# A gated-delta layer: the triangular inverses from 16x16 blocks on GpSimd and three joins on TensorE, with a wave of distance

## The reference

```
L      = -(k*beta) k^T * decay        strictly lower triangular
attn   = inverse of (I - L)
v_new  = attn (v*beta) - attn (k*beta*exp(g)) state
out    = (q*exp(g)) state + ((q k^T) * decay, lower triangular) v_new
state  = state*exp(g_last) + (k*exp(g_last - g))^T v_new
```

## Time and profile before

| | us |
|---|---|
| median of three runs | 3206.09 (3205.75 to 3207.62) |
| the profiled execution's own time | 3207.93 |
| its span | 3206.1 |

### The profile page before, as it was taken

One profiled execution on the slowest core, in us unless ns is written; L12 is line 12 of the kernel. 1 busy time (PEld: TensorE's weight loads), 2 busy tenths in 40 slices (PEclk: granted clock), 3 DMA queues, 4 the chain that ended last, 5 costly groups with the idle time before them and its releaser, 6 DMA issues. The chain is left out here.

```text
span 3206.1 us, 59779 instructions
## 1 busy us (share of the span) xinstructions
PE 2795.5 (87%) x25220; PEld 1858.5 (58%) x25220; DVE 1640.8 (51%) x3069; ACT 1096.7 (34%) x2104; POOL 222.2 (7%) x203
## 2 busy tenths in 40 slices
PE   6697999969979586589999999999999999999988
PEld 3235444435324343477777777777777777777773
DVE  1633555545531422466466556646655665665541
ACT  1261111100421221344444444444444444444431
POOL 1300111100020022000000000000000000000000
PEclk8798999989989797799999999999999999999999
DMA  1001110010010000000000000000000000000000
GB/s 44 1 0 69 40 39 25 15 31 1 1 41 0 25 25 25 11 12 11 8 11 12 8 11 15 12 8 12 12 8 12 15 11 8 11 12 8 2 5 13
DMA packets 39684, 50.31 MB, mean 16 GB/s; under 512 B 5904, under 2 KB 28816, under 8 KB 39312
## 3 DMA queue, kind: packets, MB, share of 16 engines
q1 hardware_dynamic: 39440, 46.73, 4.6%
HBM read 45.68 MB, written 1.05 MB: 15 GB/s over the span
## 5 line engine op out<-in xcount | busy, mean ns | idle before, releaser
L874 PE MATMUL ps<-all_xn,f_w 128*128 128x512 f32 x640 | 287.7, 594 | 1.9 <-ACT f_share L892 1.9
L1374 PE MATMUL ps<-all_xn,a_w_qkv 128*128 128x512 f32 x512 | 256.4, 626 | 0.0
L1801 DVE SCALAR_TENSOR_TENSOR a_qkv<-a_raw,a_cur_taps,a_qkv 128x1024 f32<-128x1024 f32 x192 | 245.6, 1279 | 1.5
L1468 PE MATMUL ps<-a_inv_half,a_powers 64*64 64x64 f32 x5120 | 219.8, 220 | 0.2 <-DVE a_inv_half L1849 0.2
L1662 ACT ACTIVATE a_powers<-ps 128x512 f32<-128x512 f32 x208 | 124.2, 597 | 260.5 <-PE ps L1460 260.5
L1849 DVE TENSOR_TENSOR a_inv_half<-a_inv_half,ps 128x256 f32<-128x256 f32 x256 | 106.8, 417 | 207.3 <-PE ps L1468 207.3
L874 PEld LDWEIGHTS ps<-all_xn,f_w 128*128 128x128 f32 x640 | 122.2, 191 | 155.8 <-issue 155.8
L1468 PEld LDWEIGHTS ps<-a_inv_half,a_powers 64*64 64x64 f32 x5120 | 186.3, 134 | 11.0 <-issue 10.6
L1782 POOL TENSOR_TENSOR a_rstd<-a_var,a_half 128x4 f32<-128x4 f32 x64 | 64.4, 1007 | 1801.2 <-DVE a_var L1883 1801.2
L897 ACT ACTIVATE f_act_h<-ps 128x512 f32<-128x512 f32 x80 | 47.8, 597 | 374.5 <-PE ps L874 374.5
L1456 PE MATMUL ps<-a_powers 64*64 64x64 f32 x3584 | 174.0, 224 | 0.3 <-DVE a_powers L1807 0.3
(11 more groups left out here) (263 smaller groups left out, 5256.9 us busy)
## 6 DMA issues: line engine op xcount, KB each, us to landing
f_w<-in_f_w SPq DMA_DIRECT2D x24, 512.0 KB, 4.5
a_w_qkv<-in_a_w SPq DMA_DIRECT2D x16, 512.0 KB, 3.7
a_w_z<-in_a_w SPq DMA_DIRECT2D x16, 256.0 KB, 2.7
a_w_out<-in_a_wo SPq DMA_DIRECT2D x16, 256.0 KB, 2.7
f_w<-in_f_w SPq DMA_DIRECT2D x24, 128.0 KB, 2.3
f_index_in<-in_f_index SPq DMA_DIRECT2D x1, 2144.0 KB, 12.1
all_x<-in_x_t SPq DMA_DIRECT2D x1, 1024.0 KB, 4.8
a_wq<-in_a_wq SPq DMA_DIRECT2D x2, 512.0 KB, 3.9
```

Of the source, the lines that this page charges most:

```text
L874: mm = pe.matmul(ps[:, bank + n % 2, :], w[:, v, k, f * P:(f + 1) * P], xn[:, k, b * T:(b + 1) * T], start=k == 0, stop=k == KC - 1)
L1374: mm = pe.matmul(ps[:, to, :], w_qkv[:, k, mt * P:(mt + 1) * P], xn[:, k, b * T:(b + 1) * T], start=k == 0, stop=k == KC - 1)
L1468: mm = pe.matmul(halves(BUP)[t, r, :], powers[t, n % 2, u, r, :], inv_half[t, r, :], start=True, stop=True)
L1801: dve.scalar_tensor_tensor(to, rows, tap, to, ALU.mult, ALU.add).then_inc(conv_ready if j == TAPS - 1 else conv_step, 1)
```

## The change

Only `delta_attention` and its constants change. Each 128x128 triangle is now inverted in blocks of 16, then joined to 32, 64 and 128.

- VectorE makes v0(w+1) as before. SyncE (`spread`) stores it whole in DRAM (256 KB), copies the blocks beside the diagonal in four small DMAs, waits for the store, and reads the eight 16x16 diagonal blocks of each matrix back with four DMAs in runs of 64 bytes, so that one block lies in one partition: 32 partitions of 256 elements.
- GpSimd (`substitute`) adds the identity and does 14 steps of forward substitution, each a multiplication and an addition that wait for each other, and then writes a transposed copy: 29 two-input instructions and one copy, each waiting for the one before.
- SyncE (`gather`) waits for that, stores the result with eight DMAs in runs of 64 bytes to DRAM, waits for them, and loads it back with one DMA of 64 KB.
- VectorE (`widen`) spreads the 16-wide blocks to 32 columns. TensorE joins: `join_a`, `close_a` (32x32 operands), `join_b`, `close_b` (32x32), `join_c`, `close_c` (64x64), with six small copies by ScalarE and VectorE and an addition between them.
- The five squarings, the five updates, the transposition of v0 and their copies are gone. The loops over heads are written out; tables of the current head's gates and taps are no longer copied.
- The recurrence of wave w-1 stays in iteration w, but its normalised output is turned and projected in iteration w+1: the loop runs from -1 to 65. Three buffers replace two for at, qg, v_row and k_row.
- The weight DMAs stand in the same SyncE queue, ahead of `gather(w)` and `spread(w+1)`, with waits for work of earlier iterations.

```diff
+                def spread(w):
+                    sp.wait_ge(v0_ready, PR * (w + 1))
+                    sp.dma_start(v_dram[w % 2, 0:P * PR * P].rearrange("(p r c) -> p r c", p=P, r=PR),
+                                 v0[:, w % 2, :, :]).then_inc(v0_stored, 16)
...
+                    for k in range(4):
+                        of = slice(k * HP, k * HP + SB)
+                        sp.dma_start(v0_off[of, w % 2, :, SB:],
+                                     v0[of, w % 2, :, k * HP + SB:(k + 1) * HP]).then_inc(off_loaded, 16)
+                    sp.wait_ge(v0_stored, 16 * (w + 1))
...
+                    for r in range(PR):
+                        sp.dma_start(l16[r * NB:(r + 1) * NB, w % 2, :].rearrange("b (j c) -> b j c", j=SB),
+                                     blocks[:, :, r, 0:SB]).then_inc(l_loaded, 16)
+                def gather(w):
+                    sp.wait_ge(sub_done, w + 1)
+                    rows = t_dram[w % 2].rearrange("(b j) k r c -> b j k r c", b=NB)
+                    for r in range(PR):
+                        for k in range(2):
+                            sp.dma_start(rows[:, :, k, r, :],
+                                         z16[r * NB:(r + 1) * NB, w % 2, k, :].rearrange("b (j c) -> b j c", j=SB)
+                                         ).then_inc(t_stored, 16)
+                    sp.wait_ge(t_stored, 128 * (w + 1))
...
+                    sp.dma_start(t_narrow[:, :, :, :], t_dram[w % 2]).then_inc(t_loaded, 16)
...
+                    if made(w):
+                        gather(w)
+                    if made(w + 1):
+                        spread(w + 1)
...
+                def substitute(w):
+                    pool.wait_ge(l_loaded, 64 * (w + 1))
...
+                    pool.tensor_tensor(z16[:, w % 2, 0, :], l16[:, w % 2, :], ident16[:, :],
+                                       ALU.add).then_inc(sub_step, 1)
+                    for j in range(1, SB - 1):
+                        n = SB - 1 - j
+                        pool.wait_ge(sub_step, steps * w + 2 * j - 1)
+                        pool.tensor_tensor(term[:, 0:j, j + 1:], z[:, 0:j, j:j + 1].broadcast_to([HP, j, n]),
+                                           rows[:, j:j + 1, j + 1:].broadcast_to([HP, j, n]),
+                                           ALU.mult).then_inc(sub_step, 1)
+                        pool.wait_ge(sub_step, steps * w + 2 * j)
+                        pool.tensor_tensor(z[:, 0:j, j + 1:], z[:, 0:j, j + 1:], term[:, 0:j, j + 1:],
+                                           ALU.add).then_inc(sub_step, 1)
+                    pool.wait_ge(sub_step, steps * (w + 1))
+                    pool.tensor_copy(z16[:, w % 2, 1, :].rearrange("p (i c) -> p i c", i=SB),
+                                     z16[:, w % 2, 0, :].rearrange("p (c i) -> p i c", c=SB)).then_inc(sub_done, 1)
...
+                def join_a(w):
+                    pe.wait_ge(widened, w + 1)
...
+                        for q in Q4:
+                            mm = pe.matmul(narrow(BW)[q, r, :], v0_off[q, w % 2, r, :], t_wide[q, 1, r, :],
+                                           start=True, stop=True)
```

More of the change, by code:

```diff
@@ L1318, in run_heads, with narrow @@
[L1318 to L1324, removed]
-        with nc.Block() as block:
[L1328 to L1338, removed]
+        def narrow(n):
+            return ps[:, n, 0:PR * HP].rearrange("p (r t) -> p r t", r=PR)
@@ L1472, in join @@
-                def join(w):
-                    pe.wait_ge(inv_ready, (LEVELS + 1) * (w + 1))
-                    pe.wait_ge(whole_ready, w + 1)
-                    first, second = HALVES
+                        for k in range(3):
+                            q, at_col = Q4[k], Q4[k % 2]
+                            mm = pe.matmul(lower(BH)[q, r, at_col], t_wide[q, 0, r, :], wa[q, r, :],
+                                           start=True, stop=True)
+                    mm.then_inc(a_psum, 1)
@@ L1605, in _ @@
                     project_z(0, n, PROJ[n % 3])
-                make(0, 0, 0, 0)
-                make_keys(0, 0, 0)
-                turn(0)
-                pe.wait_ge(zs_ready, 4)
-                run_heads(waves)
-                w = CH * KH - 1
-                corner(w, CH - 1)
-                recall(1, w, CH - 1)
-                solve(w, CH - 1)
-                answer(w, CH - 1)
-                turn_out(w)
-                project_out(KH - 1, w, CH - 1)
+                pe.wait_ge(gates_ready, 1)
+                pe.wait_ge(cleared, 2)
+                for w in range(-1, W + 2):
+                    if made(w + 1):
+                        make(w + 1)
+                    if made(w - 1):
+                        recall(w - 1)
+                    if made(w):
+                        join_a(w)
+                    part(w, 0)
+                    if made(w - 1):
+                        solve(w - 1)
+                    if made(w + 1):
+                        turn_values(w + 1)
+                    if made(w):
+                        close_a(w)
+                    part(w, 1)
+                    if made(w - 1):
+                        answer(w - 1)
+                    if made(w):
+                        join_b(w)
+                    part(w, 2)
+                    if made(w + 1):
+                        turn_keys(w + 1)
+                    if made(w):
+                        close_b(w)
+                    if made(w - 2):
+                        turn_out(w - 2)
+                    part(w, 3)
+                    if made(w):
+                        join_c(w)
+                    if made(w - 2):
+                        project_out(w - 2)
+                    if made(w):
+                        close_c(w)
             @block.scalar
@@ L1787, in _, with convolve @@
+                for w in range(-1, W + 1):
+                    if made(w + 1):
+                        substitute(w + 1)
+                    if made(w - 1):
+                        root(w - 1)
             @block.vector
             def _(dve):
-                def convolve(g, gp, mt, j):
-                    if j == 0 and mt == 0:
-                        dve.tensor_copy(cur_taps[:, :], taps[:, bass.ds(g, 1), :].rearrange("p h n -> p (h n)")
-                                        if not isinstance(g, int) else taps[:, g, :]).then_inc(taps_ready, 1)
-                        dve.wait_ge(taps_ready, g + 1)
-                    tap = cur_taps[:, mt * TAPS + j:mt * TAPS + j + 1]
-                    rows, to = raw[:, mt, :, j:j + T], qkv[:, gp, mt, :, :]
+                def convolve(g, mt, j):
+                    tap = taps[:, g, mt * TAPS + j:mt * TAPS + j + 1]
+                    rows, to = raw[:, mt, :, j:j + T], qkv[:, g % 2, mt, :, :]
```

779 lines of the change are left out of this document (375 added, 404 removed).

## The result

| | before | after |
|---|---|---|
| median of the runs, us | 3205.92 (3203.53 to 3207.62, 4 runs) | 3414.14 (3412.06 to 3421.65, 4 runs) |
| ratio, with 95% interval | | 1.0654 [1.0636, 1.0673] |
| mean wave, us | 28.2 | 30.8 |
| TensorE busy over one head from 2140 us on | 91% | 67% |

The change costs 208 us; the forecast was 236 more. The profiled execution of the new kernel took 3415.48 us, with a span of 3413.7.

What follows compares the result with a forecast made beforehand. The ring through GpSimd and DRAM was to bound the wave at 31.6 us: 64 x 31.6 + 32 - 19 = 2035 us against 1799, 236 more, so 3206 + 236 = 3442 us; range 3120 to 3790.

Steps and rivals of the forecast that it cites:

- the ring: Closed one-wave loop from widen and make_v0 through DRAM and GpSimd back to widen: 27.1 us, 31.6 with port waits.
- The stores: Eight 8 KB stores of the substitution's result to DRAM: seven issues and a landing, 3.3 + 2.0 = 5.3 us.
- v0_off hidden inside the store: SyncE's four v0_off issues, 0.47 us apart, were to end inside v0's 2.7 us store to DRAM.
- The port waits: GpSimd's substitution blocked by VectorE's conv1 to conv3 and make_qg: 4.5 us a wave, bounds 0 to 6.5.
- GpSimd's small instructions: Substitution's 29 instructions at 0.20 us fixed plus 2.09 ns an element; 11.5 us together with hand-over waits and the copy.
- The rival at 0.5 us fixed: GpSimd's small instructions cost 0.5 us fixed, making the ring 40.3 us and the time 3999 us; chance 0.18.
- Loads: DRAM reads on SyncE: four 8 KB loads of diagonal blocks at 3.4 us, the 64 KB load before widen at 2.2.
- The joins: TensorE's added 32x32 and 64x64 matmuls: 4.0 us at the 64-wide pace, 5.2 us a wave for all.
- The work loop: TensorE's work plus its wait for VectorE's make_low, make_right, make_scores and widen: 26.1 us a wave.
- TensorE's relief decides: Rival: the ring falls below 26.1 us, so the work loop sets the wave; 3109 us, chance 0.18.
- Also in the last head: Sign to look for: GpSimd's rstd rows an even 31 to 32 us apart there too, instead of about 21.
- The weight loads: SyncE's weight DMAs each cost the ring one issue, 0.47 us, three in four waves.

Runs made afterwards that it cites:

- e1: Changed kernel without the 28 instructions of the 14 substitution steps, inverses wrong in value: 2992.04 us, ratio 0.933.
- e2: Changed kernel with convolution taps 1 to 3 left out from the second head on: 3245.43 us, ratio 1.0113.
- e3: Changed kernel with the four v0_off DMAs issued behind the four diagonal-block loads, not ahead of them: 3347.7 us, ratio 1.0441.
- e4: Changed kernel with all four convolution instructions moved to the end of VectorE's iteration, nothing left out: 3314.27 us, ratio 1.0338.
- e5: Changed kernel with one store of 64 runs of 1 KB replacing eight DMAs, load back in 64 B runs: 3099.28 us, ratio 0.9692.
- e6: Changed kernel with the edits of e5 and e3 together: 3045.34 us, ratio 0.9518.
- e7: e6 plus the edit of e4 (convolution instructions at the end of VectorE's iteration): 3162.73 us, ratio 0.9886.
- e8: e6 with TensorE's projection part(w, 0) put ahead of join_a(w): 3047.42 us, ratio 0.9519.

## Why the prediction was right, and where its terms were off

The steps of the ring in all kernels but e1, in us, each the mean of the 54 turns from widen(4) to widen(58), read from the timelines of VectorE, SyncE and GpSimd:

| step | after | e2 | e3 | e4 | e5 | e6 | e7 | e8 |
|---|---|---|---|---|---|---|---|---|
| widen to v0's store | 1.5 | 1.5 | 1.5 | 1.5 | 1.5 | 1.5 | 1.5 | 1.5 |
| to the first load | 3.4 | 3.4 | 2.5 | 3.4 | 3.4 | 2.4 | 2.5 | 2.4 |
| to GpSimd's first instruction | 2.9 | 2.9 | 2.8 | 2.9 | 2.9 | 2.8 | 2.8 | 2.9 |
| substitution | 14.4 | 11.5 | 14.4 | 11.9 | 14.4 | 14.4 | 11.4 | 14.3 |
| first store to the load's issue | 7.0 | 7.1 | 7.0 | 7.1 | 1.8 | 1.8 | 2.1 | 1.8 |
| to widen | 1.8 | 1.9 | 1.8 | 2.3 | 2.3 | 2.4 | 7.0 | 2.3 |
| turn | 31.05 | 28.27 | 30.01 | 29.11 | 26.18 | 25.26 | 27.27 | 25.31 |

- **The ring bounds the wave.** Shown. Three of its links were shortened in different ways. In the table's means e2 took 2.9 us off the substitution and 2.8 off the turn, e3 1.0 off the way to GpSimd and 1.0 off the turn, e5 4.8 off the stores and the load and 4.9 off the turn. None of the three touches TensorE's work. With the mean wave T, the forecast's way of adding, 3206 + 64 T + 32 - 1799, gives 3245 for e2 (T = 28.21, measured 3245) and 3100 for e5 (T = 25.95, measured 3099). The tail of 32 us was 32.6, from the end of widen(63) at 3304.3 to 3336.9.
- **The stores: +1.7 us.** I counted 0.47 us for an issue, from the earlier trace rows. The eight took 5.64 us, 0.70 each, and the last landed behind them. The runs of 64 bytes, which the sum left out, cost nothing beyond that: from the end of the issues to the load's issue it is 1.37 us, and with e5's one store in runs of 1 KB 1.31. This is the largest miss of the sum, on the step that turned out to be the cheapest to remove.
- **v0_off hidden inside the store: wrong, +0.8.** Its four issues took 3.13 us, 2.86 in the mean, and the store 2.1 (the page of after, below). e3 shows it by itself.
- **The port waits: 3.7 us against 4.5, mechanism as told.** Shown by e2 (the work gone) and e4 (the same work elsewhere): 11.2 and 11.8 us for the substitution. conv1 to conv3, make_qg and conv0 were the ones. A piece waits only for what is left of the other's instruction, so each cost 0.3 to 1.0 us rather than its full length. And conv0 met the substitution too, which I had only in the upper bound: it has one SBUF operand that is a tensor, yet GpSimd's instruction at 2211.54 ends with it, at 0.72 us instead of some 0.25. The whole timeline of after says which instructions hold GpSimd up. Of the pieces that begin while a multiply-add of two SBUF operands runs, and at least 0.1 us before its end, 164 of 168 take over 0.35 us; beside make_qg 49 of 49, beside conv0 14 of 16. Beside carry (one operand in SBUF, one in PSUM) it is none of 129, beside the reduction of a_sq none of 65.
- **GpSimd's small instructions: 10.8 us against 11.5, right.** The line through the earlier trace rows carried from 512 elements down to 14: 0.20 forecast fixed, plus 0.03, measured 0.20 for 14 elements (0.20 to 0.23 over the four of that size). The rival at 0.5 us fixed is out. The power and the MEMSET were poor guides.
- **Loads: -0.6 and -0.4.** Issues were shorter than in the earlier trace rows (0.38 us each for the four loads) and landings shorter than in the earlier trace rows. The hand-overs' 0.4 are inside the measured steps. These misses and the substitution's cancel the stores' and v0_off's; 31.2 against 31.6 owes something to luck.
- **The joins: 5.2 us forecast, some 3.2 measured.** This term was mis-sized and not visible in the result, because TensorE wasn't the bound; e1 brought it out, 118 us below its expectation. TensorE's timeline after:

```profile
2201.80 0.65 PE L1491 MATMUL ps<-a_t_wide,a_v_off 32*32 32x32 f32 x32 [7.94 <-DVE a_t_wide L1894]
2202.38 3.78 PE L1413 MATMUL ps<-all_xn,a_w_qkv 128*128 128x512 f32 x4
...
2208.08 0.45 PE L1503 MATMUL ps<-a_t_wide,a_wa 32*32 32x32 f32 x32
2208.35 0.45 PE L1507 MATMUL ps<-a_wa,a_t_wide 32*32 32x32 f32 x24
2208.74 1.98 PE L1413 MATMUL ps<-all_xn,a_w_qkv 128*128 128x512 f32 x4
```

  The 56 records from 2208.08 to 2208.74 come every 0.012 us, below my lower bound of half of 0.031. The work loop is at most 24.3 us, not 26.1; the joins' 2.0 us cover that 1.8, and whether another term was too large as well isn't shown. The rival "TensorE's relief decides" then had a better time, 3206 + 64 x 24.3 + 32 - 1799 = 2994 or less, than the 3109 I gave it (e1: 2992), but a ring that had to fall even further.
- **"Also in the last head": wrong, and against my own sum.** Without convolutions GpSimd's first instructions are 27.9 us apart there (3255.9 to 3283.8), the substitution 11.1 us. The sum had this, as -3.8 a wave; the sentence on what to look for forgot it.
- **The weight loads** were to cost the ring one issue each. They cost it nothing: in every turn the first store begins 0.03 us after the substitution, so SyncE was through with them before. In e1, with a short substitution, they do hold the stores up.
- **TensorE's share** was forecast at 70% and is 67%. The rstd rows come every 30.9 us in the mean (2161.73 to 2285.22 for four), just under the 31 to 32 that I named.

The page of after, DMA issues, with the landings that these points use (columns as in the earlier trace rows):

```profile
a_v_dram<-a_v SPq DMA_DIRECT2D x64, 256.0 KB, 2.1
a_v_off<-a_v SPq DMA_DIRECT2D x256, 4.0 KB, 1.8
```

**Open.** Why an issue takes some 0.7 us for stores and v0_off but 0.38 for the four loads and 0.33 for the 256 KB store wasn't separated: the slow ones take data out of SBUF in pieces of 64 B, the quick ones read DRAM or write long runs. e5 changed the number of issues and the length of the runs at once, so how the 5.3 us that it saved there divide between the two is not shown.

## What to carry to other kernels

When a step leaves an engine's queue for a path through DRAM and another engine, write down the closed ring, from the instruction that feeds it to the same instruction one wave on, and compare its sum with the wave. Distance between steps hides it only if the ring has more than one wave in it; here widen and the next v0 stand in one queue, so it had one. That is read from the program; no run tried a ring with more distance. In such a ring count the issues of the queue as well as the landings: a DRAM layout that lets one DMA do the work of eight (e5), and side transfers put behind the loads (e3), made of a loss of 208 us a gain of 156. Moving VectorE's work away from GpSimd pays only while the place that it moves to is covered (e4 against e7).

## What the runs showed of the hardware

- Records of 32x32 matmuls spread over four quarters came every 0.012 us (56 from 2208.08 on, at the full clock) and every 0.018 at the lower one (32 from 2201.80 on), against 0.031 for 64-wide ones over two and 0.075 for those that share one quarter. Two records are one f32 matmul.
- An issue on SyncE's queue took 0.31 to 0.39 us for v0's store, for e5's one store and for the 64 KB load, 0.38 for each of the four loads in the turn above, 0.70 for each of the eight stores, and 0.63 to 1.0 for those of v0_off (four in 2.50 to 4.03 us over all runs). What in the transfer decides it is open, as said; the eight stores and four v0_off together took 8.8 us of a wave of 31.2.
- A 64 KB load in 1024 runs of 64 B holds the ring only 0.5 us longer than one of 512 B to a partition (3.74 against 3.28 us, e5).
- A VectorE instruction with one SBUF input can hold up GpSimd as well. conv0 (L1847, 0.75 us for 1024 elements, where the multiply-add of two inputs takes 1.28) ends at 2212.14, the GpSimd instruction beside it at 2212.26 after 0.72 us; 14 of 16 such meetings look like this. The Trainium skill, page SBUF — State Buffer, section Who interferes with whom, lists tensor_scalar among the operations whose two-port modes take the shared pair when their operands meet its conditions; the rows agree with that.
- TensorE's clock is at its lower level after its waits: after 7.94 us of idling the four projection records at 2202.38 took 3.78 us (granted clock 0.50 from 2202.40 to 2205.90), and four of the same shape at 2208.74 took 1.98 (1.00 from 2208.00 to 2208.80), the two levels of 1.2 and 2.4 GHz. In e6, with 2.74 us of idling, the first four still took 3.36. The granted clock of one head was 0.95 before and 0.81 after, and of 2000 to 2500 us 0.89 in e6. TensorE's timeline in e6:

```profile
2239.31 0.65 PE L1488 MATMUL ps<-a_t_wide,a_v_off 32*32 32x32 f32 x32 [2.74 <-DVE a_t_wide L1891]
2239.89 3.36 PE L1410 MATMUL ps<-all_xn,a_w_qkv 128*128 128x512 f32 x4
```

With a ring as the bound that costs nothing that shows: e8 has the higher clock of the two, 0.93 against 0.89, and the same time as e6. It is part of the work loop all the same.
